# Moving small matmul groups between neighbours in TensorE's order, in both attentions of a two-layer decoder kernel

## The chip, the cores and the metric

The kernel runs on one NeuronCore of one Trainium2 chip. The metric is the device time of one launch in microseconds (us), as the median of several runs.

## The reference, cut to what matters

The model is a decoder of two layers, each of which has a self-attention, a cross-attention and a mixture-of-experts part, with layer norms between. The input is 4 sequences of 256 tokens with 256 features. Only the two self-attentions are touched by the change.

```python
# layer 0: linear attention with decay, chunks of 128
q, k, v = silu(x @ Wq), silu(x @ Wk), silu(x @ Wv)        # 16 heads of 16 features
scores = einsum('bchd,bshd->bhcs', qb, kb) * D            # D: decay and causal mask
o = scores @ v (+ what the state of the chunk before gives)
gate = (x @ Wg1) @ Wg2                                    # Wg1: 256 x 16, Wg2: 16 x 256
o = o * sigmoid(gate); o = o * rsqrt(mean(o*o per head) + eps) * w
x = x + o @ Wo
...
# layer 1: softmax attention with rotary positions, causal
attn = softmax(where(causal, -inf, q @ k.T / 4)); x = x + (attn @ v) @ wo.T
```

## The kernel before, in words

Everything between the first load and the last store stays on the chip. Each engine has one program, written out by hand, and runs it in order; semaphores tie the programs together. A wait holds up all that stands behind it on its engine. TensorE (PE) writes into eight PSUM banks, VectorE (DVE) and ScalarE (ACT) read them out, so a bank must be read before PE writes it again.

A matmul of f32 operands shows as two records in the trace, so "x8" is four matmuls. The groups of matmuls have three shapes. Full ones (128*128) are the projections `queries`, `keys`, `values`, the output projection `output0` or `output`, and all transposes. Score products and `gate` contract over at most 32 rows (32*128, 16*128). Value products `mixed_values` and `mixed_probabilities`, and the inner gate `gate_inner`, have at most 32 output columns (128*32, 128*16).

**Attention of layer 0** (`attention0` on each engine). PE warms up, handles sequence 0, and then runs a loop over a = 0 to 3, with b = a - 1 and c = a + 1. The scores of sequence a come in three parts, `scores_by_key(a, 0..2)`, which all use banks 4 to 7. Before each part PE waits until DVE's `decayed` has multiplied the part before by the decay (`p_done`). Between the parts stand: the output projection of sequence a - 2, the gate of a, the value products of b, and the projections of c. A period is, on PE: scores 0, output0(a-2), gate(a), four quarters of mixed_values(b), queries(c), scores 1, keys(c), sums_of_squares(b), scores 2, gate_inner(c), values(c), transposed_tokens(c+1). Bank 0 is shared by queries, values and gate. So `gate(a)` waits for `v_ready`, which ACT sends when it has read the values of a out of bank 0. ACT's period is gate, squares, queries, keys, a load of the exp/ln table, `root` (one ln and one exp), gate_inner, a load of the silu table, values, transposed_tokens. DVE's period is decayed 0, add_out(a-2) with its norm statistics, gated_values(b), decayed 1, decayed 2, and the scaling of b. The last period (a = 3) has no projections; behind it come the last output projections and the first work of the experts.

**Attention of layer 1** (`attention1`). 24 steps, n = 0 to 23, six for each sequence. Step n has `scores_by_query(n)` into one of two pairs of banks, and the transposes of the probabilities of step n - 2 (`transposed_probabilities`). DVE takes the maximum of each row (`row_max`) and copies half of the transposes; ACT copies the other half, in `copy_transposed(n - 2)`, and only then runs its exponentials `probabilities(n)`: four of 256 columns, or eight of 128 columns where n is a multiple of 3. PE's scores of step n + 2 wait for them (`p_done`). From step 8 on, value products of the sequence before (`mixed_probabilities`, four quarters, the first two with 256 columns, the others mostly with 128) are spread over the steps: quarter 0 in steps 8, 14, 20, quarter 1 in 9, 15, 21, quarter 2 in 10, 16, 22, and quarter 3 in 13 and 19. Steps 13 and 19 also have `reciprocals_by_feature`, steps 15 and 21 the output projection.

In step 8 the first quarter waits for `q_ready`, because bank 0 still holds turned queries that ACT copies out at the end of its step 7, ahead of `copy_transposed(6)`:

```python
if b >= 0 and (turn % 2, k) == (0, 2):
    if b == 0:
        pe.wait_ge(q_ready, 2 * NB)
    mixed_probabilities(b, 0)
```

Of the kernel before, what the change touches and what calls it, by code (L numbers as in the profile page):

```python
# [22 lines left out]
NB, SEQ = 4, 256  # L23
# [57 lines left out]
def build(nc, d, out):  # L81
    with ExitStack() as ctx:
# [361 lines left out]
        def _(v):  # L444
# [121 lines left out]
            def attention0():  # L566
                for a in range(NB):
                    b = a - 1
                    decayed(a, 0)
                    if a == 0:  # L570
                        normalise(0, 2)
                    if a >= 2:
                        add_out(0, a - 2)
                        norm_statistics(1, a - 2)
                    if a >= 1:
                        gated_values(b)
                    decayed(a, 1)
                    if a == 0:
                        v.wait_ge(const_loaded, 16)
                        v.tensor_copy(identb[:, :], ident).then_inc(setup_v, 1)  # L580
                        v.tensor_copy(negqs[:, :], neg_qs).then_inc(setup_v, 1)
                        normalise(0, 3)
                    if a == NB - 1:
                        normalise(2, a - 3)
                        normalise(1, a - 2)
                        scaled(0, b)
                    decayed(a, 2)
                    if 1 <= a < NB - 1:
                        scaled(0, b)
                    if a == NB - 2:  # L590
                        blocks_output(a - 2)
                bilinear(NB - 3)
                v.wait_ge(pe_last_p0, 1)
                split_lo(0, 0, 0)
                gated_values(NB - 1)
                norm_statistics(2, NB - 3)
                add_out(0, NB - 2)
                norm_statistics(1, NB - 2)
                normalise(2, NB - 3)
                scaled(0, NB - 1)  # L600
                split_lo(0, 1, 1)
                normalise(1, NB - 2)
                tokens_low(0, 0)
                bilinear(NB - 2)
                norm_statistics(2, NB - 2)
                add_out(0, NB - 1)
                norm_statistics(1, NB - 1)
                normalise(2, NB - 2)
                blocks_output(NB - 1)
                router_maxima(0, 0)  # L610
                normalise(2, NB - 1)
                split_lo(0, 2, 2)
                weight_shared(0, 0)
                weight_shared(0, 1)
                act_low(0, 0, 0)
                tokens_low(0, 1)
                router_probabilities(0, 0)
                act_low(0, 1, 1)
                router_choice(0, 0)
# [312 lines left out]
        def _(a):  # L932
# [17 lines left out]
            def attention0():  # L950
# [19 lines left out]
                for period in range(NB):  # L970
                    b, c = period - 1, period + 1
                    if period >= 1:
                        gate(period)
                    if c == NB:
                        a.preload_act_table_set(LN_EXP)
                        norm(2, period - 3)
                        norm(1, period - 2)
                        squares(b)
                        split_hi(0, 0, 0, 0)
                        root(b)  # L980
                        split_hi(0, 1, 1, 0)
                        split_hi(0, 2, 2, 0)
                    else:
                        if period >= 1:
                            squares(b)
                        queries(c)
                        keys(c)
                        if period >= 1:
                            a.preload_act_table_set(LN_EXP)
                        if period >= 2:  # L990
                            norm(1, period - 2)
                        if period >= 1:
                            root(b)
                        gate_inner(c)
                        if period == 0:
                            links(0)
                        values(c)
                        if period == 0:
                            links(1)
                        if c + 1 < NB:  # L1000
                            transposed_tokens(c + 1, c + 1)
# [335 lines left out]
        def _(pe):  # L1337
# [39 lines left out]

            def gate_inner(b):

                if b >= 1:  # L1380
                    pe.wait_ge(k_ready, 2 * b + 2)
                for kk in range(KD):
                    last = mm(ps[0:HD, piece_bank("g1", b), 0:SEQ], wg1[:, kk, :], xT4[:, kk, b, :], kk == 0, kk == KD - 1)
                last.then_inc(pe_g1, 1)
# [7 lines left out]

            def keys(b):

                features(0, PIECE_BANK["k"], 1, b).then_inc(pe_k, 1)

            def values(b):
# [144 lines left out]
            def attention0():  # L1542
# [14 lines left out]
                for a in range(NB):  # L1557
                    b, c = a - 1, a + 1
                    pe.wait_ge(q_ready, a + 1)
                    pe.wait_ge(k_ready, 2 * a + 2)  # L1560
                    if a == 0:
                        pe.wait_ge(g1_ready, 1)
                        pe.wait_ge(v_ready, 2)
                    scores_by_key(a, 0)
                    if a >= 2:
                        output0(a - 2)
                    if a >= 1:
                        gate(a)
                    if a >= 1:
                        for quarter in range(4):  # L1570
                            mixed_values(b, quarter)
                    if c < NB:
                        queries(c)
                    if a == 0:
# [12 lines left out]
                    if a >= 1:  # L1587
                        sums_of_squares(b)
                    scores_by_key(a, 2)
                    if 1 <= a < NB - 1:  # L1590
                        gate_inner(c)
                    if c < NB:
                        values(c)
                    if c + 1 < NB:
                        pe.wait_ge(g1_ready, c + 1)
                        transposed_tokens(0, c + 1)
                mixed_values(NB - 1, 0)
                output0(NB - 2)
# [33 lines left out]
            def attention1():  # L1632
# [24 lines left out]
                for n in range(STEPS):  # L1657
                    turn, k = divmod(n, 3)
                    b = turn // 2 - 1
# [9 lines left out]
                    if n == 1:  # L1669
                        pe.wait_ge(v_ready, 4 * NB)  # L1670
                    scores_by_query(n)
                    if n < 2:
                        query_or_key(NB - 1, n)
                    if n >= 2:
# [3 lines left out]
                    if n == 7:  # L1678
                        turned(NB - 1)
                    if b >= 1 and (turn % 2, k) == (0, 1):  # L1680
                        mixed_probabilities(b - 1, 3)
                        reciprocals_by_feature(b - 1)
                    if b >= 0 and (turn % 2, k) == (0, 2):
                        if b == 0:
                            pe.wait_ge(q_ready, 2 * NB)
                        mixed_probabilities(b, 0)
                    if b >= 0 and (turn % 2, k) == (1, 0):
                        mixed_probabilities(b, 1)
                        if b >= 1:
                            output(1, b - 1)  # L1690
                    if b >= 0 and (turn % 2, k) == (1, 1):
                        mixed_probabilities(b, 2)
                transposed_probabilities(STEPS - 2)
                transposed_probabilities(STEPS - 1)
                mixed_probabilities(NB - 2, 3)
# [505 lines left out]
```

## Time and profile before

| | |
|---|---|
| median of 3 runs | 914.99 us (914.62 to 916.02) |
| profiled execution | span 913.5 us from the first to the last instruction |
| PE busy | 891.8 us, 98% of the span |
| DVE busy | 615.2 us, 67% |
| ACT busy | 423.4 us, 46% |
| mean granted TensorE clock | 0.998 of full speed |
| chain that ended last | PE 85%, DVE 7%, ACT 5% |

The profiled execution has its span, 913.5 us, and no second clock beside it; the median of the runs is 1.5 us longer, as the launch has a little around the first and the last instruction. The page's busy time of PE contains the filling and draining of the array, so "98% busy" does not say that matmuls stream for 98% of the time. How long one group of matmuls really takes is read from its start to the start of the next group.

### The profile page before, as it was taken

What the parts mean: (1) busy time and instruction counts of PE and PEld (TensorE: products, weight loads), DVE (VectorE), ACT (ScalarE), POOL (GpSimd) and SP (SyncE); (2) the same over time, 40 slices, a digit from 0 to 9 for tenths busy, and PEclk for the clock granted to TensorE, in tenths of its full rate; (3) what the DMA queues carried; (4) which work ended last, traced back from release to release, by engine and by line L of the source; (5) the groups of instructions that cost most, each with busy time, mean ns of one, the idle gap of its engine ahead of it and who ended that gap; (6) DMA issues with size and microseconds to landing.
All of it is one profiled execution on the core that took longest, in us unless ns stands there. A gap on an engine that the chain in (4) does not pass through costs nothing.

```text
span 913.5 us, 14200 instructions
## 1 busy us (share of the span) xinstructions
PE 891.8 (98%) x5377; PEld 687.2 (75%) x5377; DVE 615.2 (67%) x1185; ACT 423.4 (46%) x1063; POOL 101.2 (11%) x128
## 2 busy tenths in 40 slices
PE   8998999999999999999999999999999999999998
PEld 5665778888888876667877777777767778888886
DVE  4679656656665667656787786878776566666665
ACT  7554643333443469863543444343454443333342
POOL 4011000000000220003122232323210000000000
PEclk9999999999999999999999999999999999999999
DMA  6003111111100500006200000000010111111001
GB/s 188 1 6 119 36 52 52 37 49 52 34 1 1 218 13 1 2 1 263 90 2 1 1 1 1 1 1 2 0 36 18 36 52 52 52 38 49 17 0 47
DMA packets 12537, 37.10 MB, mean 41 GB/s; under 512 B 2080, under 2 KB 4352, under 8 KB 11712
## 3 DMA queue, kind: packets, MB, share of 16 engines
q1 hardware_dynamic: 12448, 36.32, 11.9%
q8 instruction: 37, 0.61, 0.3%
q14 instruction: 20, 0.16, 0.1%
q0 software_dynamic: 32, 0.01, 0.0%
HBM read 35.27 MB, written 1.05 MB: 40 GB/s over the span
## 4 chain that ended last, share of the span: by engine, by line
PE 85%; DVE 7%; ACT 5%; issue 1%; DMA 1%; SPq 0%; POOL 0%; DVEq 0%; ACTq 0%
PE ps L1339 79%; PE ps L1972 3%; PE ps L1512 2%; DVE P L536 1%; ACT Q L1128 1%; DMA X<-in_x 1%; DVE stats L460 1%; DVE xn L468 1%; ACT probs_q L1246 0%; ACT whi L1143 0%; DVE weighted_h L688 0%; DVE probs_q L860 0%; DVE wlo L804 0%; ACT h_hi L1173 0%; ACT silu_g L1168 0%
## 5 line engine op out<-in xcount | busy, mean ns | idle before, releaser
L1173 ACT ACTIVATE h_hi<-weighted_h 128x512 fp32r<-128x512 f32 x100 | 63.3, 633 | 152.7 <-DVE weighted_h L688 150.4
L698 DVE TENSOR_TENSOR h_lo<-weighted_h,h_hi 128x512 fp32r<-128x512 f32 x100 | 69.3, 693 | 66.1 <-ACT h_hi L1173 66.0
L1339 PE MATMUL ps<-xT_first,whi 128*128 128x512 f32 x376 | 111.3, 397 | 1.2 <-ACT silu_g L1168 1.2
L1339 PE MATMUL ps<-xT_second,whi 128*128 128x512 f32 x376 | 108.4, 391 | 1.3 <-ACT silu_g L1168 1.2
L725 DVE TENSOR_TENSOR shared_gate<-silu_g,row_shares 128x512 f32<-128x512 f32 x88 | 60.9, 692 | 63.5 <-ACT silu_g L1168 63.4
L1168 ACT ACTIVATE silu_g<-ps 128x512 f32<-128x512 f32 x100 | 59.5, 596 | 75.8 <-PE ps L1339 75.5
L1339 PE MATMUL ps<-xT,merged_q 128*128 128x256 f32 x384 | 91.9, 384 | 0.0
L1331 POOL TENSOR_TENSOR latent_rot<-rope_buf 128x256 f32<-128x256 f32 x96 | 68.4, 733 | 180.2 <-DVE rope_buf L815 180.2
L1339 PEld LDWEIGHTS ps<-xT_first,whi 128*128 128x128 f32 x376 | 70.3, 188 | 19.0 <-issue 2.8
L1339 PEld LDWEIGHTS ps<-xT_second,whi 128*128 128x128 f32 x376 | 70.1, 188 | 17.0 <-issue 2.5
L1339 PE MATMUL ps<-h_hi,wlo 128*128 128x512 f32 x200 | 78.5, 392 | 0.0
L1339 PEld LDWEIGHTS ps<-xT,merged_q 128*128 128x128 f32 x384 | 70.5, 190 | 10.5
L1339 PE MATMUL ps<-h_hi,whi 128*128 128x512 f32 x188 | 74.7, 397 | 0.7 <-DVE h_lo L698 0.7
L1339 PE MATMUL ps<-h_lo,whi 128*128 128x512 f32 x188 | 73.3, 390 | 0.0
L1246 ACT ACTIVATE probs_q<-ps,neg_max 128x256 f32<-128x256 f32 x128 | 58.8, 472 | 28.7 <-DVE neg_max L850 28.7
L688 DVE TENSOR_TENSOR weighted_h<-ps,shared_gate 128x512 f32<-128x512 f32 x88 | 60.9, 692 | 10.2
L1339 PE MATMUL ps<-xT_first,wlo 128*128 128x512 f32 x200 | 62.8, 396 | 0.0
L1339 PE MATMUL ps<-xT_second,wlo 128*128 128x512 f32 x200 | 61.7, 390 | 0.0
L1128 ACT ACTIVATE Q<-ps,nm 128x256 f32<-128x256 f32 (+1 forms) x128 | 52.4, 448 | 2.4 <-DVE nm L545 2.4
L860 DVE TENSOR_SCALAR probs_q<-probs_q,rsum 128x256 f32<-128x256 f32 x128 | 49.9, 452 | 1.1
L1339 PE MATMUL ps<-latent_rot,merged_s 128*64 128x256 f32 (+1 forms) x256 | 47.4, 386 | 0.0
L1339 PEld LDWEIGHTS ps<-latent_rot,merged_s 128*64 128x64 f32 (+1 forms) x256 | 32.1, 163 | 19.3 <-issue 14.5
(197 smaller groups left out, 1572.8 us busy)
## 6 DMA issues: line engine op xcount, KB each, us to landing
raw<-in_ffn SPq DMA_DIRECT2D x50, 384.0 KB, 3.1
wx<-in_wx SPq DMA_DIRECT2D x4, 2048.0 KB, 10.9
cx<-in_cx SPq DMA_DIRECT2D x1, 1536.0 KB, 6.6
X<-in_x SPq DMA_DIRECT2D x4, 256.0 KB, 6.9
kvc<-in_kvc SPq DMA_DIRECT2D x1, 1024.0 KB, 14.4
out<-X SPq DMA_DIRECT2D x4, 256.0 KB, 2.2
wqkv<-in_wqkv SPq DMA_DIRECT2D x1, 768.0 KB, 8.3
wqkv<-in_wqkv SPq DMA_DIRECT2D x1, 512.0 KB, 6.4
```

The source lines that it names most:

```text
L688: v.tensor_tensor(weighted_h[:, u % 2, :], ps[:, 5 + u % 2, :], gate[:, u % 2, :], ALU.mult).then_inc(weighted[l], 1)
L698: v.tensor_tensor(h_lo[:, u % 2, :], weighted_h[:, u % 2, :], h_hi[:, u % 2, :].bitcast(F32), ALU.subtract).then_inc(act_lo[l], 1)
L725: v.tensor_tensor(shared_gate[:, u % 2, :], silu_g[:, u % 2, :], row_shares[:, hf, :], ALU.mult).then_inc(gated[l], 1)
L860: last = v.tensor_scalar(probs_q[:, w % 2, st, ab, pair, :], probs_q[:, w % 2, st, ab, pair, :], rsum[:, st, ab, pair:pair + 1], None, ALU ...
L1128: last = a.activation(Q[:, n % 3, i, width * h:width * h + width], step_scores(n)[:, i, width * h:width * h + width], ACT.Exp, bias=nm[:, ...
L1168: a.activation(silu_g[:, u % 2, :], ps[:, gate_bank(n), :], ACT.Silu).then_inc(silu_done[l], 1)
L1173: a.activation(h_hi[:, u % 2, :], weighted_h[:, u % 2, :], ACT.Copy).then_inc(act_hi[l], 1)
L1246: last = a.activation(probs_q[:, w % 2, st, ab, pair, :], ps[:, xscore_bank(ab), 256 * pair:256 * pair + 256], ACT.Exp, bias=neg_max[:, st ...
L1331: g.tensor_tensor(latent_rot[:, TILE_ORDER[j], part, :], r1[:, j, 256 * part:256 * part + 256], r2[:, j, 256 - 256 * part:512 - 256 * part ...
L1339: return pe.matmul(o, l, r, start=start, stop=stop, skip_group_check=True)
L1512: last = pe.transpose(ps[:, bank, 128 * c:128 * c + 128], src, ident)
L1972: last = pe.transpose(ps[:, turned_bank(ab), 256 * pair + 128 * st:256 * pair + 128 * st + 128], probs_q[:, w % 2, st, ab, pair, 128 * lt: ...
```

## The change

Only the order of instructions changes; no instruction is added or removed. In the attention of layer 0, from a = 1 on, `gate(a)` comes directly behind scores 0, then the value products, then the inner gate of c (which stood behind scores 2), then the output projection of a - 2. The waits move with them: the inner gate waits for the copied tokens, `keys` for the copied inner gate, and the next transposes for the copied keys. DVE does gated_values(b) ahead of add_out(a-2), and ACT copies the inner gate ahead of the squares. In the attention of layer 1 each quarter of value products comes between the scores of its step and the transposes, where it stood behind the transposes.

```diff
 # DVE, attention0
                     if a == 0:
                         normalise(0, 2)
+                    if a >= 1:
+                        gated_values(b)
                     if a >= 2:
                         add_out(0, a - 2)
                         norm_statistics(1, a - 2)
-                    if a >= 1:
-                        gated_values(b)
                     decayed(a, 1)
...
 # ACT, attention0
                         if period >= 1:
+                            gate_inner(c)
                             squares(b)
                         queries(c)
                         keys(c)
...
                         if period >= 1:
                             root(b)
-                        gate_inner(c)
                         if period == 0:
+                            gate_inner(c)
                             links(0)
                         values(c)
...
 # PE
             def gate_inner(b):
-                if b >= 1:
+                if b == 1:
                     pe.wait_ge(k_ready, 2 * b + 2)
+                elif b >= 2:
+                    pe.wait_ge(xt_ready, b + 1)
...
             def keys(b):
+                if b >= 2:
+                    pe.wait_ge(g1_ready, b + 1)
...
                     scores_by_key(a, 0)
+                    if a >= 1:
+                        gate(a)
+                        for quarter in range(4):
+                            mixed_values(b, quarter)
+                    if 1 <= a < NB - 1:
+                        gate_inner(c)
                     if a >= 2:
                         output0(a - 2)
-                    if a >= 1:
-                        gate(a)
-                    if a >= 1:
-                        for quarter in range(4):
-                            mixed_values(b, quarter)
                     if c < NB:
                         queries(c)
...
                     scores_by_key(a, 2)
-                    if 1 <= a < NB - 1:
-                        gate_inner(c)
                     if c < NB:
                         values(c)
                     if c + 1 < NB:
-                        pe.wait_ge(g1_ready, c + 1)
+                        if c == 1:
+                            pe.wait_ge(g1_ready, c + 1)
+                        else:
+                            pe.wait_ge(k_ready, 2 * c + 2)
                         transposed_tokens(0, c + 1)
...
 # PE, attention1
                     scores_by_query(n)
+                    if b >= 0 and (turn % 2, k) == (0, 2):
+                        if b == 0:
+                            pe.wait_ge(q_ready, 2 * NB)
+                        mixed_probabilities(b, 0)
+                    if b >= 0 and (turn % 2, k) == (1, 0):
+                        mixed_probabilities(b, 1)
+                    if b >= 0 and (turn % 2, k) == (1, 1):
+                        mixed_probabilities(b, 2)
+                    if b >= 1 and (turn % 2, k) == (0, 1):
+                        mixed_probabilities(b - 1, 3)
                     if n < 2:
                         query_or_key(NB - 1, n)
                     if n >= 2:
...
                     if b >= 1 and (turn % 2, k) == (0, 1):
-                        mixed_probabilities(b - 1, 3)
                         reciprocals_by_feature(b - 1)
...
+                    if b >= 1 and (turn % 2, k) == (1, 0):
+                        output(1, b - 1)
```

## Rows read from the trace of the kernel before

**Rows 1.** The page, busy time of each engine and share of the span.
```profile
PE 891.8 (98%) x5377; PEld 687.2 (75%) x5377; DVE 615.2 (67%) x1185; ACT 423.4 (46%) x1063; POOL 101.2 (11%) x128
```

**Rows 2.** Timeline, PE, period a = 1: start us, us, engine, what, count.
```profile
30.28 1.17 PE L1339 MATMUL ps<-qk 32*128 32x128 f32 x32 [0.21 <-DVE P L536]
31.25 1.02 PE L1339 MATMUL ps<-g1S,wg 16*128 16x256 f32 x4
32.20 2.81 PE L1339 MATMUL ps<-P,vpad 128*32 128x256 f32 x64
...
37.94 1.99 PE L1339 MATMUL ps<-xT,wqkv 128*128 128x256 f32 x8
```

**Rows 3.** Timeline, PE, period a = 2 and the start of a = 3.
```profile
45.12 1.18 PE L1339 MATMUL ps<-qk 32*128 32x128 f32 x32
46.23 1.99 PE L1339 MATMUL ps<-wo,on 128*128 128x256 f32 x8
48.15 1.13 PE L1339 MATMUL ps<-g1S,wg 16*128 16x256 f32 x4
49.21 2.81 PE L1339 MATMUL ps<-P,vpad 128*32 128x256 f32 x64
51.94 1.99 PE L1339 MATMUL ps<-xT,wqkv 128*128 128x256 f32 x8
...
54.94 1.99 PE L1339 MATMUL ps<-xT,wqkv 128*128 128x256 f32 x8
...
57.73 1.15 PE L1339 MATMUL ps<-qk 32*128 32x256 f32 x16
...
61.69 1.17 PE L1339 MATMUL ps<-qk 32*128 32x128 f32 x32
...
68.51 1.15 PE L1339 MATMUL ps<-qk 32*128 32x256 f32 x16
```

**Rows 4.** Timeline, ACT and DVE of attention 0, periods a = 1 to 3.
```profile
45.47 0.66 ACT L1047 ACTIVATE vpad<-ps 128x256 f32<-128x256 f32 x2
...
62.90 0.66 ACT L1047 ACTIVATE vpad<-ps 128x256 f32<-128x256 f32 x2
...
66.67 0.74 DVE L515 TENSOR_TENSOR X<-X,ps 128x256 f32<-128x256 f32 x2
...
67.99 0.30 DVE L463 BATCH_NORM_AGGREGATE mv<-stats 128x2 f32<-128x6 f32 x2
...
69.73 2.36 DVE L536 TENSOR_TENSOR P<-ps,DT 128x1024 f32<-128x1024 f32 x2 [0.39 <-PE ps L1339]
```

**Rows 5.** Timeline, PE, attention 1, steps 8 to 10.
```profile
349.68 1.09 PE L1512 MATMUL ps<-cst,Q 128*128 128x128 f32 x8
351.09 1.07 PE L1339 MATMUL ps<-P,vpad 128*32 128x256 f32 x16 [0.32 <-ACT qk L1108]
...
353.72 1.09 PE L1512 MATMUL ps<-cst,Q 128*128 128x128 f32 x8
354.74 1.07 PE L1339 MATMUL ps<-P,vpad 128*32 128x256 f32 x16
355.74 0.39 PE L1339 MATMUL ps<-negqs,identb 128*128 128x256 bf16 x2
...
358.15 0.64 PE L1339 MATMUL ps<-P,vpad 128*32 128x128 f32 x16
```

**Rows 6.** Timeline, ACT, attention 1, steps 8 to 10.
```profile
351.32 0.57 ACT L1128 ACTIVATE Q<-ps,nm 128x256 f32<-128x256 f32 x1
...
353.02 0.32 ACT L1128 ACTIVATION_READ_ACCUMULATOR Q<-ps,nm 128x1 f32 x1
...
354.85 0.60 ACT L1139 ACTIVATE P<-ps 128x512 f32<-128x512 f32 x1 [1.50 <-PE ps L1512]
...
358.26 0.60 ACT L1139 ACTIVATE P<-ps 128x512 f32<-128x512 f32 x1
```

**Rows 7.** Windows behind attention 0: stretch, length, busy of PE, PEld, DVE, ACT, POOL; PEclk.
```profile
80.00:84.00 4.00, 3.18 (x12) 2.37 (x11) 3.81 (x12) 2.91 (x7) 1.24 (x2) 0.66 0.15 60
```

More of the change, by code:

```diff
@@ L1680, in attention1 @@
                     if b >= 1 and (turn % 2, k) == (0, 1):
-                        mixed_probabilities(b - 1, 3)
                         reciprocals_by_feature(b - 1)
[L1683 to L1692, printed above, removed]
+                    if b >= 1 and (turn % 2, k) == (1, 0):
+                        output(1, b - 1)
                 transposed_probabilities(STEPS - 2)
```

## The prediction

> **What bounds the kernel now.** I read the page first: PE is busy for 98% of the span, the next engine for 67% [rows 1]. So PE's program sets the time, and the order of its groups can only matter in three ways: what a change of shape between neighbours costs, whether PE arrives at a wait too early, and what it releases later for others. None of the three is in a busy time. I therefore went to the timeline of PE through both attentions and took intervals from start to start, and then to the same stretch of ACT and DVE, to see how near the waits are to being late. The reader should see two things. First, in attention 0 PE runs on without a gap in periods 1 and 2 [rows 2, 3], but ACT reads the values out of bank 0 at 45.47 to 46.13, while the gate that waits for it starts at 48.15 [rows 3, 4]. The cover is 2 us, and 1.92 of that is the output projection that stands ahead of the gate. Second, in attention 1 ACT has a cycle of its own: transposes, copy, exponentials, scores two steps later.
>
> **The change part by part: what a change of shape costs.** Four full matmuls of 256 columns take 1.92 us where both neighbours have another shape (46.23 to 48.15) [rows 3]. Scores 0 take 1.11 us ahead of the output projection and 0.97 ahead of the gate; the gate takes 1.06 behind the output projection and 0.95 behind scores [rows 2, 3]. So a border between two shapes costs 0.11 on either side, 0.22 in all, when full matmuls or scores are next to it. In attention 1 the transposes take 1.02 ahead of a value quarter, and the quarter 1.00; transposes that are followed by full work take 0.93 by my reading of the other steps (2.41 from one step's start to its quarter holds the 1.02) [rows 5]. There a removed border gives 0.1, or 0.2 where an output projection or the reciprocals then stand directly behind the transposes.
>
> The Trainium skill, "TensorEngine Tiling (Array Packing)", section Key Properties, says that changing the tiling mode drains TensorE while changing the tile within a mode does not. The rows agree (1.11 against 0.97), and by that rule alone the sum would be the gains below without the waits, -2.5 us.
>
> **Attention 0, gains.** The gate behind the scores saves one border at a = 2 and a = 3, the output projection beside the queries saves one at a = 2, the inner gate beside the value products saves the border that it had on one side. The inner gate with value products is shown nowhere: before they cost 2.74 and some 0.97 (the gate, of the same size, has 0.95) [rows 2], together 3.71; without any border or filling it would be 3.41. I take 3.53, since the fill at the start and the drain at the end remain. PE alone would gain 0.15 + 0.6 + 0.25 = 1.0 us over the three periods.
>
> **Attention 0, waits.** I walk the new order with the measured intervals.
> Period 1: scores 0 at 30.28, gate 31.25, value products 32.20, +3.53 inner gate included, queries 35.73, +3.00 (queries and scores 1, 51.94 to 54.94) keys 38.73, which is 0.79 later than the 37.94 of before; +2.79 scores 2 at 41.52 [rows 2, 3]. Scores 2 to the end of DVE's decay is 1.22 + 2.36, with 0.05 for the semaphore 3.62 (I take it from scores 1 at 68.51 and the decay at 69.73) [rows 3, 4]. Before, PE had the inner gate to fill this time. Now scores 0 of a = 2 waits until 45.14; it was 45.12. The gain of period 1 is gone.
> ACT is the next to be late. From the start of keys to the end of the values' read it took 46.13 - 37.94 = 8.19 us, without a pause: two silus, table load, ln, exp, inner gate copy, table load, values. Without the moved copy it is shorter; I count 0.25, an estimate from the values' two reads of as many columns, 0.66 together. So `v_ready` comes at 46.67, and the gate, at which PE arrives at 46.11, goes at 46.72.
> Period 2: gate 46.72, +1.06 products 47.78, +3.53 output projection 51.31, +3.63 (1.92 + 1.93 less one border) scores 1 at 54.94, +1.08 keys 56.02 against 54.94 before, +2.79 scores 2 at 58.81, +3.62 scores 0 of a = 3 at 62.43 (61.69 before) [rows 3]. ACT's chain was 63.56 - 54.94 = 8.62, less the same 0.25 [rows 4], so the values are read at 64.39 and gate(3) goes at 64.43, 1.02 later than PE gets there (63.40).
> Period 3: +1.06 + 2.73 + 1.92 gives scores 1 at 70.13; it was 68.51 [rows 3]: 1.62 later.
> DVE then adds to this. Before, add_out(1) with its statistics (66.67 to 68.29) was over before scores 1 [rows 4]. Now the output projection ends directly ahead of scores 1: add_out starts at 70.24, takes 1.54 with the statistics, and the decay starts at 71.78 instead of 69.73: 2.05 late. Queued behind it are the normalising of the next parts, the scaling and the third decay. ACT's squares of b = 2 stand behind the norm that needs these statistics, so the root and the scaling come 0.3 later still. From 69.73 on the chain that ended last runs through DVE, with no other slack that I find. I take 2.35 us lost for attention 0.
> What covers this term: nothing but the output projection could stand ahead of the gate. Bounds: 1.6 (DVE's part is absorbed), 2.7 (3.71 instead of 3.53, twice).
>
> **Attention 1, gains.** Eleven quarters move. Seven are plain (0.1 each), two gain 0.2 with the output projection, two with the reciprocals: 1.5 us [rows 5]; one of the seven is the quarter of step 8, counted below, so 1.4 for steps 9 to 22.
>
> **Attention 1, the wait of step 8.** The first quarter went at 351.09, 0.32 after the transposes were done, released by ACT's copy of the queries [rows 5]. That copy stands behind ACT's exponentials of step 7 and does not move. Now the quarter stands ahead of the transposes: PE would be there at 349.68 and waits 1.41. Then quarter 1.00, transposes 0.93, next step at 353.02; it was 352.09. Loss 0.93.
>
> **Attention 1, ACT's cycle.** The copy comes 1.13 after the transposes start (353.72 to 354.85). The copy and eight exponentials take 3.41 (354.85 to 358.26), the copy and four exponentials some 0.49 + 2.02 (351.32 to 353.34) [rows 5, 6]. With 0.05 to release PE the cycle from transposes to the scores two steps on is 4.6 us where n is a multiple of 3, else 3.7. PE's cover is transposes (0.93) and the whole next step; before it was also the quarter, which now stands ahead of the transposes. A step without a quarter is 2.3, a narrow quarter 0.57 (0.64 less the overlap of 0.07), the reciprocals 0.45. So step 9 has 0.93 + 2.3 + 0.57 = 3.8 against 4.6; steps 12 and 18 have 4.3 against 4.6; steps 10 and 16 have 3.25 against 3.7. Walked forward, as each wait gives cover to the next, PE's new waits are 0.75, 0.2, 0.3, 0.43 and 0.3 = 2.0, less 0.25 that it waits there before: 1.7.
> Sum: 0.93 + 1.7 - 1.4 = 1.2 to 1.4 lost; DVE's row_max of step 17 behind the statistics pushes to the upper end. I take 1.4. Bounds: -0.4 if the cycle never shows, 2.2 if DVE's copies are late too.
>
> The Trainium skill, the same page, section PSUM Bottleneck, says that tiling speeds up TensorE but not the reading of PSUM, which may become the bound. Both waits above are of that kind; that rule and my walk agree.
>
> **Clock.** Behind attention 0 there is a stretch where PE had little to do from 76 to 80, and the granted clock was 0.66 in 80 to 84 [rows 7], so part of it at 1.2 instead of 2.4 GHz. That cost about 1 us (the output projection there takes 2.4 instead of 1.9, the transposes as much more). The stretch stays, later; I take the same cost and a bound of 1 us to both sides.
>
> **Sum.** 913.5 + 2.35 + 1.4 = 917.25 for the profiled execution. The median of the runs was 1.5 above that span, so 914.99 + 3.75 = 918.7 us.
>
> **Rivals.**
> Faster: PE's borders are all that counts, 1.0 + 1.5, because ACT and DVE follow as soon as they are released and their chains shorten with PE. Place: both attentions; price -1.0 - 1.5, so 912.5. It holds if `v_ready` is there when PE arrives at the gate, which needs ACT's chain to be 0.6 us (a = 2) and 1.0 us (a = 3) shorter than measured, and q_ready 1.4 earlier. Against it: the chain has no pause to give. By what the Trainium skill (the page and section above) says of draining, taken alone, this is the case to come.
> No change: attention 0's loss is absorbed in the stretch behind it, where PE has pauses, and attention 1 gives its 1.4 less 0.4 for better luck: 916.0; with a clock that doesn't fall, 915.
> Only attention 0 loses and attention 1 comes out even (its cycle has more slack than I count): 917.3, still slower.
>
> **Chances.** The forecast and its neighbour with one attention even: 0.73. Within 0.2% (1.8 us, about what a measurement of this kernel can tell from no change; 913.2 to 916.8): 0.15. Faster: 0.12. The range goes from 915.0, in the middle of the second case, to 920.8 (both upper bounds, 918.7 + 0.35 + 0.8 + clock 1.0).
>
> **What would show it.** Right, if PE waits for ACT's vpad (v_ready) before the gates of a = 2 and 3, 0.6 and 1.0 us; scores 0 of a = 3 starts at about 62.4; the decay of (3, 1) is behind DVE's statistics at 71.8; PE waits about 1.4 us in step 8 for ACT's qk, and some 0.2 to 0.8 for ACT's Q in steps 11, 14, 18 and 20. Wrong, if the gates start without a wait, or if the value products followed by the inner gate take well under 3.4 us, since tiles then overlap in a way that no row of before shows.

## The result, and the profile after

The changed kernel takes 921.48 us (median of 4 runs, 919.52 to 922.82), beside 915.04 us for the kernel before (median of 4, 914.62 to 916.02). The ratio is 1.0070, 95% interval 1.0058 to 1.0082. It is slower, as forecast, but by 6.4 us instead of 3.75; 921.48 lies 0.7 above the range. In the runs below, one of the kernel before (1656 us, mean clock 0.84) and one of e6 (1584 us, 0.72) were in a far slower state and are left out of every number.

The profiled execution has a span of 919.3 us, 5.8 more than before. The page, busy times and then the chain that ended last:

```profile
PE 892.6 (97%) x5377; PEld 689.0 (75%) x5377; DVE 616.1 (67%) x1185; ACT 422.8 (46%) x1063; POOL 101.3 (11%) x128
...
PE 83%; ACT 8%; DVE 7%; issue 1%; POOL 0%; DVEq 0%; ACTq 0%
```

PE's busy time grew by 0.8 us [rows 1], the span by 5.8: PE waits more. ACT's share of the chain went from 5% to 8%.

The timeline of PE in attention 0, from a = 1 to scores 1 of a = 3 and a first group of the experts behind it. The bracket at the end is idle time and what ended it.

```profile
29.68 1.18 PE L1340 MATMUL ps<-qk 32*128 32x128 f32 x32 [0.21 <-DVE P L536]
...
31.60 2.81 PE L1340 MATMUL ps<-P,vpad 128*32 128x256 f32 x64
34.23 1.03 PE L1340 MATMUL ps<-xT,wg 128*16 128x256 f32 x4
35.19 2.00 PE L1340 MATMUL ps<-xT,wqkv 128*128 128x256 f32 x8
...
40.97 1.15 PE L1340 MATMUL ps<-qk 32*128 32x256 f32 x16
...
44.68 1.18 PE L1340 MATMUL ps<-qk 32*128 32x128 f32 x32 [0.21 <-DVE P L536]
46.26 1.10 PE L1340 MATMUL ps<-g1S,wg 16*128 16x256 f32 x4 [0.40 <-ACT vpad L1048]
47.29 2.81 PE L1340 MATMUL ps<-P,vpad 128*32 128x256 f32 x64
...
62.09 1.17 PE L1340 MATMUL ps<-qk 32*128 32x128 f32 x32 [0.64 <-DVE P L536]
64.08 1.10 PE L1340 MATMUL ps<-g1S,wg 16*128 16x256 f32 x4 [0.82 <-ACT vpad L1048]
65.11 2.81 PE L1340 MATMUL ps<-P,vpad 128*32 128x256 f32 x64
67.85 2.00 PE L1340 MATMUL ps<-wo,on 128*128 128x256 f32 x8
69.77 1.15 PE L1340 MATMUL ps<-qk 32*128 32x256 f32 x16
...
114.90 0.60 PE L1755 MATMUL ps<-cst,comb 128*16 128x128 f32 x4
```

Both gates now wait for ACT's read of the values, which no gate did in [rows 3], and scores 0 waits for DVE's decay. This execution comes to scores 0 of a = 1 0.60 us earlier than [rows 2], so times are compared from there.

DVE at a = 3 after the change: the residual add and its statistics end directly ahead of the decay, as the prediction has it.

```profile
69.88 0.75 DVE L515 TENSOR_TENSOR X<-X,ps 128x256 f32<-128x256 f32 x2 [1.21 <-PE ps L1340]
...
71.21 0.30 DVE L463 BATCH_NORM_AGGREGATE mv<-stats 128x2 f32<-128x6 f32 x2
71.43 2.32 DVE L536 TENSOR_TENSOR P<-ps,DT 128x1024 f32<-128x1024 f32 x2
```

The timeline of PE in attention 1, step 8, and the first row of step 23:

```profile
351.26 0.39 PE L1340 MATMUL ps<-negqs,identb 128*128 128x256 bf16 x2 [0.31 <-ACT Q L1129]
351.58 1.13 PE L1340 MATMUL ps<-qk 32*128 32x256 f32 x8
354.05 1.90 PE L1340 MATMUL ps<-P,vpad 128*32 128x256 f32 x16 [1.34 <-ACT qk L1109]
355.88 1.89 PE L1517 MATMUL ps<-cst,Q 128*128 128x128 f32 x8
357.61 0.60 PE L1340 MATMUL ps<-negqs,identb 128*128 128x512 bf16 x2
...
405.26 0.38 PE L1340 MATMUL ps<-negqs,identb 128*128 128x256 bf16 x2
```

Windows of the same execution (stretch, length, busy of PE, PEld, DVE, ACT, POOL, then PEclk, the granted clock):

```profile
80.00:84.00 4.00, 2.73 (x6) 1.40 (x7) 3.69 (x13) 1.75 (x4) 1.41 (x2) 0.64 0.31 98
...
352.00:356.00 4.00, 2.66 (x25) 1.01 (x22) 1.63 (x2) 2.00 (x9) 0.00 (x0) 0.77 0.01 2
356.00:360.00 4.00, 4.00 (x42) 3.07 (x42) 1.68 (x3) 2.19 (x8) 0.00 (x0) 0.80 0.02 4
```

The forecast wait for ACT's `qk` is there with 1.34 us. What was not forecast stands behind it. The quarter takes 1.83 from start to start and the transposes 1.73, where they took 1.00 and 1.02 [rows 5]. The granted clock is 0.77 and 0.80 in these two windows, so part of them ran at 1.2 instead of 2.4 GHz: in finer windows the clock is 1.00 up to 354.0, 0.65 in 354.0 to 354.5 and 0.50 behind that, so it fell just as the wait ended.

**Where 5.8 us went.** To place losses I use two intervals in every profile: from scores 0 of a = 1 to the group `ps<-cst,comb` (attention 0 and the stretch behind it), and from the start of step 8 to that of step 23. Their ends in the kernel before, which [rows 2, 5] don't have:

```profile
111.94 0.60 PE L1747 MATMUL ps<-cst,comb 128*16 128x128 f32 x4
...
348.30 0.39 PE L1339 MATMUL ps<-negqs,identb 128*128 128x256 bf16 x2 [0.30 <-ACT Q L1128]
...
399.46 0.39 PE L1339 MATMUL ps<-negqs,identb 128*128 128x256 bf16 x2
```

Before: 111.94 - 30.28 = 81.66 and 399.46 - 348.30 = 51.16. After: 114.90 - 29.68 = 85.22 and 405.26 - 351.26 = 54.00. From `comb` to step 8 both take 236.36 us, from step 23 to the end both 514.04. So -0.60 (the earlier start) + 3.56 + 2.84 = 5.80, all of it. How each part divides into order and clock is what the experiments are for.

### The profile page after: what moved, and what is told of

Same layout as the page of the kernel before. It is cut to its first block, busy times and chain, and to the rows that moved or that the text cites. A ratio compares the mean times of both kernels' runs of the same rounds, so it can differ in the third digit from the quotient of the medians.

```text
span 919.3 us, 14200 instructions
## 1 busy us (share of the span) xinstructions
PE 892.6 (97%) x5377; PEld 689.0 (75%) x5377; DVE 616.1 (67%) x1185; ACT 422.8 (46%) x1063; POOL 101.3 (11%) x128
## 4 chain that ended last, share of the span: by engine, by line
PE 83%; ACT 8%; DVE 7%; issue 1%; POOL 0%; DVEq 0%; ACTq 0%
PE ps L1340 77%; PE ps L1980 3%; ACT Q L1129 2%; PE ps L1517 2%; DVE stats L460 1%; DVE P L536 1%; ACT DT L944 1%; DVE xn L468 0%; ACT probs_q L1247 0%; ACT whi L1144 0%; DVE weighted_h L688 0%; DVE X L515 0%; DVE probs_q L860 0%; ACT P L1140 0%; ACT rms L1030 0%
```

## The experiments

A fall, below, is a stretch in which the granted clock goes from 2.4 to 1.2 GHz. Two theories of the excess. **Order**: the new waits cost more than the prediction counted. **Clock**: the waits cost what was forecast, and the excess comes from falls of the granted clock behind them. The lengths of the two intervals, from the rows of each profile (A: attention 0 and behind; B: steps 8 to 23), with the medians:

| kernel | median us (runs) | ratio, 95% | A | B |
|---|---|---|---|---|
| before | 914.9 to 915.2 | 1 | 81.66 | 51.16 |
| after | 921.48 (4) | 1.0058 to 1.0082 | 85.22 | 54.00 |
| e1_second_only | 917.90 (10) | 1.0016 to 1.0036 | 81.68 | 54.00 |
| e2_first_only | 918.17 (7) | 1.0028 to 1.0058 | 84.24 | 51.16 |
| e3_step8_back | 921.81 (5) | 1.0029 to 1.0074 | 88.17 | 51.50 |
| e4_step8_filled | 922.02 (4) | 1.0064 to 1.0097 | 85.18 | 52.46 |
| e5_output_ahead | 915.90 (10) | 0.9993 to 1.0012 | 82.89 | 51.19 |
| e6_tail_filled | 915.22 (9) | 0.9992 to 1.0012 | 81.64 | 51.16 |
| e7_waits_filled | 918.96 (5) | 1.0024 to 1.0052 | 84.25 | 52.50 |
| e8_six_quarters | 914.30 (10) | 0.9982 to 1.0001 | 81.64 | 50.58 |
| e9_output2_later | 914.15 (11) | 0.9983 to 1.0001 | 81.46 | 50.57 |
| e10_all_but_step8 | 915.54 (10) | 0.9999 to 1.0018 | 81.66 | 51.50 |
| e11_second_filled | 917.36 (7) | 1.0010 to 1.0032 | 82.61 | 52.50 |
| e12_first_filled | 917.55 (7) | 1.0015 to 1.0038 | 84.23 | 51.17 |

A and B are of one profiled execution, the median is over all; where the clock falls in some executions only, they need not agree. Spans are 1.8 us below the times (918.12 and 916.3 in e1, for instance). e1 to e8 ran on one chip (kernel before: 915.16 for e1 to e4, 915.12 for e5 to e8), e9 to e12 on another (914.91); each is set against the kernel before on its own chip.

### One attention at a time

Edit of e1: the kernel before with the changes in `attention1` alone. Edit of e2: with those in `attention0` alone.

> The change in the attention of layer 1 alone (attention 0 as before). My theory: 0.9 us from the quarter of step 8 ahead of its wait, 1.6 us because TensorE's granted clock falls there (the quarter takes 1.83 instead of 1.00, the transposes 1.73 instead of 0.93), 0.3 net from ACT's cycle in steps 9 to 23: +2.8 us, 917.8. Rival, order and waits without the clock: +1.2 to +1.4, 916.4. Rival, PE's borders alone: -1.5, 913.5.

> The change in the attention of layer 0 alone. My theory: waits of the gate and of scores 0 and DVE's later statistics make 2.3 us up to the third decay of a = 3, and the stretch behind it loses about another 1 us at the lower clock: +3.4 us, 918.4. Rival, waits alone: +2.35, 917.4. If the two attentions are independent, the excess of this one and of the second alone add up to 6.4.

Attention 1 alone gives 917.90 - 915.16 = +2.7 us, attention 0 alone +3.0. Both lose, and attention 1 loses twice what was forecast (1.4). Together that is 5.7 of the 6.4 us. e2's median met its expectation, but not for the reason given: its profiled execution has a clock of 1.00 behind attention 0, and A is 84.24 without any fall. In e1, B is 54.00 as in the changed kernel. Its ten executions fall into two groups by the recorded clock: spans of 913.9 to 914.7 at 0.998 or more (three), and 915.8 to 916.7 at 0.995 to 0.997 (seven). One and the same program has two times, and the faster one is near the forecast. The profiled execution belongs to the slower group and has the fall in step 8 (0.97 and 0.61 in 348 to 356). e2 does it too: five spans of 915.1 to 916.4 at 0.997 or more, two of 919.6 and 919.7 at 0.994; neither of these two is the profiled one.

### Step 8: put back, or filled

Edit of e3, in the changed kernel: the quarter of step 8 back behind the transposes.

```diff
-                    if b >= 0 and (turn % 2, k) == (0, 2):
-                        if b == 0:
-                            pe.wait_ge(q_ready, 2 * NB)
+                    if b >= 1 and (turn % 2, k) == (0, 2):
                         mixed_probabilities(b, 0)
...
+                    if b == 0 and (turn % 2, k) == (0, 2):
+                        pe.wait_ge(q_ready, 2 * NB)
+                        mixed_probabilities(b, 0)
```

Edit of e4, in the changed kernel: three full matmuls of 256 columns into a free bank, whose result nothing reads, in the time that PE waits. The order stays as it is.

```diff
...
                         if b == 0:
+                            pe.wait_ge(k_turned, 4)
+                            for filler in range(3):
+                                mm(ps[:, 1, 0:256], ident, k_of_constants("dist"), True, True)
                             pe.wait_ge(q_ready, 2 * NB)
```

> The changed kernel with one quarter of value products (step 8) back behind the transposes. My theory: its own wait costs 0.9 and the fall of the clock that follows it 1.6, so 2.5 us come back and another 0.5 as ACT's cycle isn't late in step 11: 921.5 - 3 = 918.5; the windows around step 8 show full clock. Rival, the wait alone: -0.9, 920.6. Rival, the clock falls anyway somewhere in this attention since PE is idle more often: -1.4, 920.1.

> The changed kernel with three full matmuls of 256 columns (1.3 us, their result is not used) in the wait of step 8, nothing else. The wait itself stays as long. My theory, idle PE brings the clock down there: quarter and transposes take 1.00 and 0.93, -1.6 us, 919.9. Rival, the longer quarter and transposes come from the wait or from the new neighbours and not from the clock: no change or 0.1 slower, 921.5.

Both medians missed, 921.81 and 922.02, no better than the changed kernel. The intervals say why for e3, and for e4 in part. B behaved: 51.50 in e3, 52.46 in e4. With work in the wait, 1.54 of the 2.84 us are gone though the wait for ACT is as long. e3's profiled execution lost the time in attention 0 instead, which the edit doesn't touch: A is 88.17, 3.93 more than in e2. e4's profiled execution is its fastest (918.3, 0.998; two others have 921.1 and 921.2 at 0.994), so where its slower ones lost the time no trace shows. Timeline of PE in e3 at the gate of a = 3, then its windows:

```profile
64.46 1.75 PE L1340 MATMUL ps<-g1S,wg 16*128 16x256 f32 x4 [0.82 <-ACT vpad L1048]
66.13 5.35 PE L1340 MATMUL ps<-P,vpad 128*32 128x256 f32 x64
71.41 2.07 PE L1340 MATMUL ps<-wo,on 128*128 128x256 f32 x8
```

```profile
64.00:68.00 4.00, 3.54 (x24) 1.88 (x28) 3.77 (x8) 2.06 (x4) 0.00 (x0) 0.60 0.02 5
68.00:72.00 4.00, 4.00 (x54) 2.57 (x47) 0.45 (x1) 0.64 (x3) 0.00 (x0) 0.55 0.95 286
```

The gate waits the same 0.82 us as in the changed kernel's profile; then gate and value products take 6.95 us (64.46 to 71.41) instead of 3.77 (64.08 to 67.85). In windows of half a microsecond the clock is 1.00 up to 64.5, 0.77 in 64.5 to 65 and 0.50 from there to 71.5: it fell at the start of the gate, which therefore takes 1.67 from start to start instead of 1.03, and stayed low through the value products. Three of e3's five executions have spans of 920.0 to 920.3 at 0.993 or 0.994, the other two 915.6 and 915.9 at 0.998. This fall comes in part of the executions. Up to the last squares it costs 3.28 us ((84.91 - 30.05) - (82.07 - 30.49), against e2); a second fall at these squares (0.66 in 84 to 88) makes up the rest of the 3.93. The two groups of e2 lie as far apart, 919.6 and 916.3.

### One attention each, with its waits filled

Edit of e11: e1 with the three matmuls of e4 in step 8. Edit of e12, shown here: e2 with unused matmuls in every wait that the change made in attention 0. `filler(bank, count, rows, width)` issues `count` matmuls over `rows` rows (128 if not given) and `width` columns (256 if not given) into a free bank.

```diff
...
+                    if a == NB - 1:
+                        filler(2, 1)
                     scores_by_key(a, 0)
+                    if a >= 2:
+                        pe.wait_ge(rms_ready, a - 1)
+                        filler(1, a - 1, 32, 128 if a == 2 else 256)
                     if a >= 1:
                         gate(a)
...
+                    if a == NB - 1:
+                        filler(2, 1)
                     if a >= 1:
                         sums_of_squares(b)
...
+                filler(6, 3)
                 sums_of_squares(NB - 1)
```

> The change in attention 1 alone, with 1.3 us of full matmuls in the wait of step 8 (attention 0 as before, so its waits cannot disturb the clock). My theory: the fall of the clock goes, the wait stays: 917.9 - 1.6 = 916.4, and step 8 to step 9 takes 4.75 instead of 5.8 to 6.3. Rival, what is late in step 8 isn't the clock: 917.9.

> The change in attention 0 alone, with the same fillings as before in its waits. My theory: only order and waits are left, 2.35 to 2.8 us: 917.7, and no execution near 921. Rival, executions near 921 stay, then they don't come from PE being idle.

e11, timeline of PE at the last squares of attention 0, in step 8 and at step 23, and its windows; the fillers are the group `ps<-cst`:

```profile
79.37 2.08 PE L1347 MATMUL ps<-sq,cst 128*128 128x512 f32 x2 [1.72 <-ACT sq L1025]
...
350.79 1.56 PE L1347 MATMUL ps<-cst 128*128 128x256 f32 x6
352.28 1.07 PE L1347 MATMUL ps<-P,vpad 128*32 128x256 f32 x16
353.28 1.09 PE L1520 MATMUL ps<-cst,Q 128*128 128x128 f32 x8
354.21 0.59 PE L1347 MATMUL ps<-negqs,identb 128*128 128x512 bf16 x2
...
401.90 0.38 PE L1347 MATMUL ps<-negqs,identb 128*128 128x256 bf16 x2
```

```profile
352.00:356.00 4.00, 4.00 (x48) 2.57 (x50) 1.21 (x4) 1.74 (x7) 0.00 (x0) 1.00 0.02 4
```

Quarter and transposes are back at 1.00 and 0.93, the clock is 1.00, and B is 52.50, which is 51.16 + 1.34. Step 8 to step 9 takes 4.81, expected 4.75. But the median, 917.36, is 1 us above what I expected and only 0.5 below e1: three executions have spans of 914.1 to 914.6, four 915.6 to 916.5, beside three and seven in e1. So the times of e11 do not show that the fall went; its profile does, for one execution, which is one of the slower four for another reason. In it the clock fell behind attention 0 (0.91 in 76 to 80, 0.66 in 80 to 84), and A is 82.61, 0.93 more than in e1, although attention 0 is that of the kernel before: the last squares fell into it and took 2.08.

e12, timeline of PE at the gate of a = 3, and the group `comb`:

```profile
63.35 1.02 PE L1348 MATMUL ps<-cst 32*128 32x256 f32 x4
64.44 1.10 PE L1348 MATMUL ps<-g1S,wg 16*128 16x256 f32 x4
65.47 2.81 PE L1348 MATMUL ps<-P,vpad 128*32 128x256 f32 x64
...
114.27 0.60 PE L1770 MATMUL ps<-cst,comb 128*16 128x128 f32 x4
```

All seven executions have spans of 915.3 to 915.9; the 919.6 of e2 doesn't occur (e2 ran on the other chip). The order of attention 0 costs 917.55 - 914.91 = 2.6 us with the clock out of play, and A says the same, 84.23 - 81.66 = 2.57.

### All waits filled

Edit of e7: the changed kernel with the fillers of e11 and e12 together.

> The changed kernel with matmuls whose result is unused in each of PE's new waits: 0.2 us ahead of gate(2), 0.85 ahead of gate(3), 0.43 ahead of scores 0 of a = 3 and of the squares of b = 2, 1.3 ahead of the last squares, 1.3 in step 8. The waits keep their ends. My theory, what exceeds the predicted sum is the clock: full clock in all windows of both attentions, 915.2 + 3.75 = 918.9 at most, spread under 1.5 us. Rival, the excess is in waits that the prediction missed: 921.5, no change.

918.96, which is 3.84 above the kernel before (915.12), with more work on PE than the changed kernel has. Four of five executions have spans of 916.6 to 917.4 at a clock of 0.999 or 1.0, below all four of the changed kernel (917.7 to 921.0 at 0.994 or 0.995). The fifth, the profiled one, has 920.6, and its falls are where nothing was filled: in 16 to 20, and here, behind PE's waits of 1.38 and 0.44 us for DVE at the end of attention 1, which the kernel before has too (1.26 and 0.44, at a clock of 1.00 in its profile):

```profile
408.00:412.00 4.00, 2.85 (x16) 2.43 (x16) 1.92 (x4) 2.42 (x9) 0.00 (x0) 0.78 0.01 4
412.00:416.00 4.00, 4.00 (x45) 3.04 (x48) 2.09 (x7) 1.97 (x6) 0.00 (x0) 0.80 0.00 0
```

### The fall that the kernel before has

Edit of e6: the kernel before with four unused full matmuls ahead of the last squares of attention 0, where PE has its longest wait in this attention (1.72 us).

```diff
...
+                for filler in range(4):
+                    mm(ps[:, 6, 0:256], ident, k_of_constants("dist"), True, True)
                 sums_of_squares(NB - 1)
```

> The kernel before with four full matmuls of 256 columns (1.7 us, result unused) in the 1.72 us in which PE waits for the squares of the last sequence. Theory of the prediction, the lower clock behind attention 0 costs the kernel before 1 us: -0.5 to -1, 914.4. Rival, DVE and not PE sets the time in that stretch, so the lower clock there costs nothing before: 0 to +0.1, 915.2.

The clock is 1.00 in 80 to 84, where [rows 7] have 0.66, and nothing is gained: 915.22 against 915.12, A 81.64 against 81.66. e1 and e10 say the same without any filler: their attention 0 is that of the kernel before, the clock happens to stay at 1.00 in 80 to 84, and A is 81.68 and 81.66. So the 1 us that the prediction ascribes to this fall isn't there in the execution that it was read from: the fall began at 81.3, behind the squares, and the chain that ended last goes from the squares over ACT and DVE. It depends on the place. Before, and then in the changed kernel, where the squares themselves fall into it (clock 0.54 in 81 to 82, 0.50 in 82 to 84):

```profile
79.28 1.13 PE L1339 MATMUL ps<-sq,cst 128*128 128x512 f32 x2 [1.72 <-ACT sq L1025]
```

```profile
81.27 2.08 PE L1340 MATMUL ps<-sq,cst 128*128 128x512 f32 x2 [1.72 <-ACT sq L1026]
```

They take 2.08 instead of 1.13, ACT and DVE wait for them, and A is 85.22, against 84.24 in e2 with the same order and no fall: 0.98 us. This is not tied to the new order: e11 has the old one and loses 0.93 in the same way, and e2 has the new one and no fall behind the same wait of 1.72 us. Of the profiles, three of four with the new order (changed kernel, e3, e4, but not e2) and one of five with the old one (e11, but not the kernel before, e1, e8, e10) have the squares in a fall.

### What covered the gate

Edit of e5: e2 with the output projection and DVE's add_out back ahead of the gate; the inner gate stays beside the value products.

> Attention 0 changed, but with the output projection (and DVE's add_out) back ahead of the gate and the value products; the inner gate stays beside the value products. Attention 1 as before. My theory, the cover of the wait for the values is what the move took away: no wait before the gates, only the one of scores 0 of a = 3 for the decay stays (0.6 us): +0.5 us against before, 915.7, and no executions near 921. Rival, the inner gate's move is what costs (its copy, its waits): 918, as with the whole change in attention 0.

915.90, 2.3 us better than e2 and 0.8 above the kernel before (915.12). Timeline of PE:

```profile
63.44 1.99 PE L1340 MATMUL ps<-wo,on 128*128 128x256 f32 x8
65.36 1.13 PE L1340 MATMUL ps<-g1S,wg 16*128 16x256 f32 x4
```

With the 1.92 us of the output projection ahead of it the gate of a = 3 no longer waits. That projection was its cover. All ten executions have spans of 913.5 to 914.7, so none is in a slower group like e2's. A is 82.89 here, since the profiled execution is the slowest of the ten and its last squares are in a fall (0.57 in 80 to 84, squares 1.62).

### The parts of attention 1, and a better version

Edit of e10: e1 without the quarter of step 8. Edit of e8: the kernel before, with only the quarters of steps 13, 14, 15, 19, 20 and 21 ahead of the transposes, those whose steps have cover to spare.

```diff
                     scores_by_query(n)
+                    early = {13: (0, 3), 14: (1, 0), 15: (1, 1), 19: (1, 3), 20: (2, 0), 21: (2, 1)}.get(n)
+                    if early:
+                        mixed_probabilities(*early)
...
```

Edit of e9: e8, and in attention 0 at a = 2 alone the output projection behind the value products and `gated_values` ahead of `add_out`; the inner gate stays behind scores 2.

> Attention 0 as before; in attention 1 ten of the eleven quarters move, the one of step 8 stays behind the transposes. My theory: borders saved 1.4, ACT's cycle gives 1.7 back: +0.3 to +0.4, 915.5. Rival, step 8 had nothing to do with the loss and it stays at +2.8 as with the whole change of attention 1.

> Attention 0 as before; in attention 1 only the six quarters of steps 13, 14, 15, 19, 20 and 21 go between scores and transposes. My theory, these have cover for ACT's cycle, each saves its border (2 x 0.1, 2 x 0.2 with the output projection, 2 x 0.2 with the reciprocals), some 0.2 goes to the waits of steps 14 and 20: -0.6 us, 914.6. Rival, every quarter ahead of the transposes delays ACT by its own length and that comes back: +0.3 or more.

> The six quarters of the run before in attention 1, and in attention 0 only this: at a = 2 the gate and the value products come ahead of the output projection (DVE's gated_values ahead of add_out there); the inner gate stays behind scores 2, a = 3 stays as before. My theory: at a = 2 the inner gate keeps the values' read early enough (46.18 against PE's 46.11), so three borders less: 0.35 to 0.45 us more than the six quarters alone, 913.9. Rival, DVE's add_out and statistics come later and delay the decay of a = 2: no gain or 0.3 lost, 914.3 to 914.6.

PE's waits from 330 (325 for the changed kernel) to 425, in e10, the changed kernel and e8, the row on ACT's copies of transposes (total us, times, longest):

```profile
PE ps L1339 <- ACT Q L1128: 1.6, 5, 0.6
```

```profile
PE ps L1340 <- ACT Q L1129: 1.5, 5, 0.6
...
PE ps L1340 <- ACT qk L1109: 1.3, 1, 1.3
```

```profile
PE ps L1339 <- ACT Q L1128: 0.5, 2, 0.3
```

e10 has 915.54 (+0.6) and B = 51.50, +0.34; ten quarters moved bring no gain, since ACT's cycle takes it. e8 has the waits of the kernel before (0.5 us) and B = 50.58, -0.58; its median is 914.30, 0.8 below 915.12. e9 has 914.15 against 914.91, again 0.8. A is 81.46, so the move at a = 2 gave 0.2, under my estimate, and the medians don't show it. These two are the fastest versions tried, but at a ratio of 0.9992 with intervals up to 1.0001 a gain over the kernel before isn't shown by the medians; over the changed kernel both are ahead by 7 us.

## Why the prediction was right on the order and too low on the clock

**Attention 0, waits: right.** From scores 0 of a = 1, gate(2) goes at 16.58 (46.26 - 29.68; forecast 46.72 - 30.28 = 16.44), scores 0 of a = 3 at 32.41 (32.15), scores 1 of a = 3 at 40.09 (39.85), decay(3, 1) at 41.75 (41.50). Both gates wait as forecast: from scores 0 to the gate it is 1.58 and 1.99 instead of 0.97, so 0.61 and 1.02 (forecast 0.6 and 1.0; the brackets, 0.40 and 0.82, count from the modelled end of scores 0). The values of a = 2 are read by ACT 7.93 after the start of keys, forecast 7.94:

```profile
38.19 2.00 PE L1340 MATMUL ps<-xT,wqkv 128*128 128x256 f32 x8
...
45.46 0.66 ACT L1048 ACTIVATE vpad<-ps 128x256 f32<-128x256 f32 x2
```

The value products with the inner gate take 3.59 (31.60 to 35.19), forecast 3.53. The whole is 2.58 where I had 2.35. The missing 0.2 is mostly scores 2 to scores 0, which took 3.71 twice (40.97 to 44.68, 58.38 to 62.09) instead of 3.62.

**Attention 1: right in sum, its two halves both too large.** Step 8 costs 52.50 - 51.50 = 1.00 us (forecast 0.93). ACT's cycle made 1.6 - 0.5 = 1.1 us of new waits (forecast 1.7), and ten quarters gained 1.1 - 0.34 = 0.76 (forecast 1.4): some 0.1 for each, as the six of e8 did (0.58), and not 0.2 beside an output projection or the reciprocals. The errors cancel: 1.34 measured, 1.4 forecast.

**Sum of the order: right.** 2.58 + 1.34 = 3.9 by the intervals, 3.84 by e7, forecast 3.75. That it is so close owes something to luck, as the errors inside attention 1 cancel.

**Clock: the step that failed.** "The stretch stays, later; I take the same cost and a bound of 1 us to both sides." I looked at the one fall that the kernel before shows, and didn't ask whether the new waits make new ones. They do: at step 8 (54.00 - 52.50 = 1.50 us), and at the gate of a = 3 (3.3 us, in part of the executions). The fall behind attention 0, which cost the kernel before nothing in its profile, costs 0.98 in that of the changed kernel, because the squares are in it; whether the new order makes that more frequent or it was this execution's luck is open. The profiled execution adds up: -0.60 + 2.58 + 0.98 + 1.34 + 1.50 = 5.80. The median of +6.4 isn't resolved further, since only one of its four executions (spans 917.7 to 921.0, clocks 0.994 and 0.995) has a trace; that the others differ by such falls is likely and not shown. With most of the falls filled away (e7) it is inside the range, at 918.96. That the cost of a fall was wrong also for the kernel before (1 us claimed, none by e1, e6 and e10) shows that the price of a lower clock can't be read from longer matmuls alone; it has to be on the path.

**The rivals.** That only the borders count fell: ACT's chain shortened by no more than the moved copy (8.19 to 7.93, 8.62 to 8.35), and both gates waited. The Trainium skill, "TensorEngine Tiling (Array Packing)", section Key Properties, says that a change of tiling mode drains TensorE. The runs agree that a border costs time, some 0.1 us for each quarter moved in e8. What decided here is nearer to what the same page says in its section PSUM Bottleneck, that the copy out of PSUM may become the bound: the waits of 0.61, 1.02 and 1.34 us are all for ACT's reads of PSUM. That attention 1 comes out even without the clock fell too (B is +1.34). "No change" fell: nothing behind attention 0 took up its loss (the interval from `comb` to step 8 is the same 236.36 us).

**Left open.** Which executions have a fall, and where, I can't say beforehand; the same program shows both. That the wait in step 8 brings its fall about rests on profiles: with fillers and the order unchanged, B is 52.46 to 52.50 in all three (e4, e7, e11), without them 54.00 in both (changed kernel, e1). That the waits ahead of the gate of a = 3 do so rests on times: a slower group in e2 (two of seven) and e3 (three of five), none with fillers in e7 (five; the profiled one lost its time elsewhere) and e12 (seven, on the other chip), and none in e5 (ten), where the gate has its cover back. Only one execution with this fall has a trace. Why e11 still has four slower executions is known for the profiled one alone, and why e3 and e4 were no faster than the changed kernel in the median isn't shown either, beyond the chance of which executions have a fall.

## What to carry to other kernels

A group ahead of a wait is cover, even if nothing says so: before moving it, find the last wait behind it and by how much its releaser is done early (here 2 us at the gate, of which 1.92 were the output projection). When an edit gives the bounding TensorE a new wait of about 1 us, price the clock as well as the wait, as a range with two likely values, with and without the fall; to test it, put unused matmuls into the wait and leave the order alone. Compare whole groups of executions by their recorded clock, since the profiled one may be of either kind, and a fall in it need not come from the edit.

## What the runs showed of the hardware

I had not expected so short a wait to bring the clock down. It fell from 2.4 to 1.2 GHz behind a wait of 1.34 us (352 to 360: 0.77 and 0.80) and, in e3, behind waits of 0.65 and 0.82 us two microseconds apart (64 to 72: 0.60 and 0.55); value products of 2.74 us then took 5.28. A wait of this size doesn't always do it: behind the same 1.72 us ahead of the last squares of attention 0 the clock stayed at 1.00 in e1, e2 and e10 and fell in the changed kernel, e3, e4 and e11. The Trainium skill, "TensorE: Matmul & The Clock Gate", section "A second HAM failure mode: psum-queue depth-cycling", tells of a kernel in which TensorE is idle shortly and often between groups of matmuls, so that the clock swings; these traces agree that short idles can be enough, with single falls behind one or two waits.

A fall costs by its place: 1.50 us in step 8, 3.28 at the gate of a = 3, 0.98 and 0.93 with the last squares in it, and nothing where it began behind them. More work can be faster: the fillers of e7 bring PE's busy time from 892.6 to 897.5 us, and it is 2.5 us faster in the median than the changed kernel (918.96 against 921.48, where the kernel before had 915.12 and 915.04).
